# Four attention blocks on one core: q and k in fp32 over 128 channels, heads in four row groups, maxima by a matmul of their own

## The reference

```python
h = group_norm(x, 32 groups) * gn_w + gn_b        # eps 1e-5; 1e-6 in the last block
q, k, v = wq h + bq, wk h + bk, wv h + bv         # per token, 128 -> 128
p = softmax(q^T k / sqrt(d))                      # blocks 0-2: 8 heads, d = 16; block 3: 1 head, d = 128
x = wp (p v) + bp + x
```

## Time and profile before

| | |
|---|---|
| runs | 115.41, 115.49, 114.85 us |
| profiled execution, first to last instruction (span) | 112.7 us; its own run time is not listed beside it |
| instructions | 2178 |
| PE matmuls, weight loads | 99.7 us (88%), 80.1 us (71%), 774 each |
| DVE, ACT, POOL busy | 77.9 us (69%), 78.4 us (70%), 7.9 us (7%) |
| mean granted TensorE clock | 0.997 |
| moved by DMA | 2.12 MB, 16 engines' mean share above a half only in two of the first three of 40 slices |

### The profile page before, as it was taken

One profiled execution on the slowest core, in us unless ns is written; L12 is line 12 of the kernel. 1 busy time (PEld: TensorE's weight loads), 2 busy tenths in 40 slices (PEclk: granted clock), 3 DMA queues, 4 the chain that ended last, 5 costly groups with the idle time before them and its releaser, 6 DMA issues.

```text
span 112.7 us, 2178 instructions
## 1 busy us (share of the span) xinstructions
PE 99.7 (88%) x774; PEld 80.1 (71%) x774; DVE 77.9 (69%) x192; ACT 78.4 (70%) x168; POOL 7.9 (7%) x17
## 2 busy tenths in 40 slices
PE   6999689979969998599999899979998898789891
PEld 6998468756955967378877678768977565579770
DVE  5467789273992879826699357997869516786862
ACT  4387569998677937989828996377999995024520
POOL 8421000000001000010000100010000000102000
PEclk9999999999999999999999999999999999999998
DMA  2950000000000000000000000000000000000011
GB/s 65 333 214 0 0 0 6 0 0 0 3 9 0 0 0 0 0 0 6 0 0 0 0 6 0 0 0 0 6 0 0 0 0 9 0 3 0 0 47 47
DMA packets 1882, 2.12 MB, mean 19 GB/s; under 512 B 336, under 2 KB 1232, under 8 KB 1872
## 3 DMA queue, kind: packets, MB, share of 16 engines
q1 hardware_dynamic: 1584, 1.84, 4.8%
q10 hardware_dynamic: 288, 0.15, 0.6%
HBM read 1.73 MB, written 0.26 MB: 18 GB/s over the span
## 4 chain that ended last, share of the span: by engine, by line
PE 58%; ACT 20%; DVE 14%; issue 4%; DVEq 0%; ACTq 0%
ACT probs L668 9%; PE ps_o L563 9%; PE ps_t L550 9%; ACT q_heads L658 8%; PE ps_w L492 7%; PE ps_o L469 6%; DVE neg_max L761 6%; PE ps_w L520 4%; PE ps_w L510 4%; PE ps_w L511 3%; PE ps_m L498 2%; DVE q_heads L755 2%; PE ps_m L537 2%; PE ps_m L477 2%; PE ps_m L609 2%
## 5 line engine op out<-in xcount | busy, mean ns | idle before, releaser
L761 DVE TENSOR_REDUCE neg_max<-ps_w 128x2 f32<-128x512 f32 x48 | 31.0, 685 | 6.8 <-PE ps_w L520 6.7
L668 ACT ACTIVATE probs<-ps_t 128x512 f32<-128x512 f32 x48 | 27.5, 597 | 4.1 <-PE ps_t L550 3.3
L550 PE MATMUL ps_t<-q_heads,k_pairs 128*128 128x256 f32 x96 | 20.8, 313 | 3.1 <-ACT probs L668 1.6
L520 PE MATMUL ps_w<-k_pairs,q_heads 128*128 128x256 f32 x96 | 20.4, 314 | 1.8 <-DVE neg_max L761 0.8
L658 ACT ACTIVATE q_heads<-ps_m 1x256 fp32r<-1x256 f32 x48 | 17.9, 373 | 5.0 <-PE ps_m L537 4.1
L550 PEld LDWEIGHTS ps_t<-q_heads,k_pairs 128*128 128x128 f32 x96 | 14.1, 189 | 7.0 <-ACT q_heads L658 4.3
L520 PEld LDWEIGHTS ps_w<-k_pairs,q_heads 128*128 128x128 f32 x96 | 13.9, 189 | 5.5 <-issue 2.4
L510 PE MATMUL ps_w<-qk_high,select 128*128 128x256 f32 x48 | 12.9, 300 | 0.9 <-DVE qk_low L726 0.5
L563 PE MATMUL ps_o<-probs,v_heads 128*32 128x256 f32 x192 | 12.8, 385 | 0.9 <-ACT probs L668 0.9
L511 PE MATMUL ps_w<-qk_low,select 128*128 128x256 f32 x48 | 11.8, 279 | 0.0
L423 POOL TENSOR_TENSOR grp<-grp,const 128x1 f32<-128x1 f32 x8 | 4.5, 558 | 93.8 <-DVE grp L715 93.8
(11 more groups left out here) (62 smaller groups left out, 130.2 us busy)
## 6 DMA issues: line engine op xcount, KB each, us to landing
w<-in_w SPq DMA_DIRECT2D x4, 256.0 KB, 4.9
xs<-in_x SPq DMA_DIRECT2D x2, 128.0 KB, 3.1
selections<-in_selections SPq DMA_DIRECT2D x1, 256.0 KB, 4.0
out<-xs SPq DMA_DIRECT2D x4, 64.0 KB, 1.6
const<-in_constants ACTq DMA_DIRECT2D x1, 137.0 KB, 3.1
vec<-in_vectors ACTq DMA_DIRECT2D x1, 12.0 KB, 3.5
```

The costliest lines, as they stand in the source:

```text
L520: last = mm(ps_w[w_slot[step]][:, qc * T:(qc + 1) * T], q_heads[b][:, i, qc * CHUNK:(qc + 1) * CHUNK], k_pairs[b][:, i // 2, :], start=Tru ...
L550: last = mm(dst, k_pairs[b][:, pair, keys], q_heads[b][:, i, :], start=True, stop=True)
L668: nc.scalar.activation(probs[:, i, :, :].rearrange("p c t -> p (c t)"), src, ACT.Exp, scale=SCALE).then_inc(exps_done, 1)
L761: nc.vector.tensor_reduce(neg_max[b][:, i // 2, :, QUAD * (i % 2)], ps_w[w_slot["scores", l, b, i]][:, :].rearrange("p (c t) -> p c t", c= ...
```

## The change

The planner goes; the file holds a fixed list (`PLAN`) of the same form of steps in one order, and each step that fills PSUM names its banks out of eight that all kinds share. Before a PE step fills a bank it waits for the step that emptied it (`bank_free`). The steps change as follows.

- Statistics: `sum_x` on DVE at the start only (later the residual accumulates the sum as it writes x), `negate_sum` on DVE, `sum_squares` on ACT (Square with accumulation, over x and two padding columns that carry eps), one fp32 `group_means` matmul. variance, power on POOL and normalise as before.
- q and k stay fp32 in 128 channels, with no high and low parts and no placing. k is stored twice: `store_k_even` (ACT) with the channels of odd heads zeroed, `store_k_odd` (DVE) with those of even heads zeroed. A group of 32 rows holds an even and an odd head, so a matmul over 32 rows gives one head's scores. `scores` and `scores_t` work on four heads at once, in four row groups and four PSUM banks, each 8 fp32 matmuls (K = 32).
- Maxima: four heads' maxima are laid in columns 0, 32, 64, 96 of `neg_max`, one `turn_max` transposes them for four heads (two transposes), `store_max` (ACT) copies 128x256 to `max_rows` (fp32r), and `add_max` adds them into the four banks of scores_t by four fp32r matmuls (K = 32, 512 columns) with a matrix whose first row of each group is ones.
- `attend` as before, but `probs` is one tile per image. Its result is transposed in 32x32 blocks by DVE (`turn_out`), divided, transposed back by DVE (`turn_back`), without ACT and PE. v's bias is folded into the output's bias (`fold_out`, `add_out`), so `store_attended` goes.
- `store_v` is on ACT. In the last layer wp wv is multiplied once (`fold_wv`, `store_wv`), so the layer has no `project_out`.
- Start: x of image 1 is issued by ACT between constants (67 KB in place of 137 KB) and vectors; SP issues x of image 0, w0, an identity of 64 KB, w1 to w3 and wv of the last layer. The selections (256 KB) and their four ACT steps go. POOL's memsets are ten. Filler matmuls are 9, none after the start.

Cut to its core:

```diff
-mm(dst, select[:, pair, 2 * k, :], qk_high[b][:, k, :], start=True, stop=False)
-last = mm(dst, select[:, pair, 2 * k + 1, :], qk_low[b][:, k, :], start=False, stop=True)
...
+elif kind == "scores":
+    bank_free(step)
+    pe.wait_ge(q_stored, nth("store_q", l, b))
...
+    keys = k_odd[b] if i else k_even[b]
+    for qc in range(NCH):
+        for g in range(PER):
+            of = slice(ROWS * g, ROWS * (g + 1))
+            last = mm(ps(*step, g)[:, qc * T:(qc + 1) * T], q[b][of, qc * CHUNK:(qc + 1) * CHUNK],
+                      keys[of, :], start=True, stop=True)
+    last.then_inc(scores_done, 1)
+elif kind == "scores_t":
...
+    for kc in range(NCH):
+        for g in range(PER):
+            of = slice(ROWS * g, ROWS * (g + 1))
+            mm(ps(*step, g)[:, kc * T:(kc + 1) * T], keys[of, kc * CHUNK:(kc + 1) * CHUNK], q[b][of, :],
+               start=kc == 0, stop=False, skip_group_check=True)
+elif kind == "add_max":
...
+    pe.wait_ge(max_stored, nth("store_max", l, b, i))
+    for g in range(PER):
+        of = slice(ROWS * g, ROWS * (g + 1))
+        dst = ps("scores_t", l, b, i, g)[:, :].rearrange("p (c t) -> p c t", c=NCH)
+        row = max_rows[b][of, i:i + 1, :].to_broadcast([ROWS, NCH, T])
+        last = mm(dst, first_rows[of, :], row, start=False, stop=True, skip_group_check=True)
+    last.then_inc(max_added, 1)
...
+elif kind == "sum_squares":
+    nc.scalar.activation(squares[b][:, 0:cols], xs[b][:, 0:cols], ACT.Square,
+                         accum_out=mom[b][:, 2:3]).then_inc(x_squared, 1)
+elif kind == "store_k_even":
+        last = nc.scalar.activation(k_even[b][:, :], src, ACT.Identity,
+                                    bias=bias[:, l, FK_EVEN:FK_EVEN + 1], scale=even)
+elif kind == "store_max":
+    nc.scalar.activation(max_rows[b][:, i, :], ps("turn_max", l, b, i)[:, 0:T],
+                         ACT.Copy).then_inc(max_stored, 1)
...
+elif kind == "store_k_odd":
+    ts(k_odd[b][:, :], ps("project_k", l, b)[:, 0:T], bias[:, l, FK:FK + 1], odd,
+       ALU.add, ALU.mult).then_inc(k_odd_stored, 1)
+elif kind == "turn_out":
+    dve.wait_ge(attended, nth("attend", l, b, i))
+    nc.vector.transpose(turned[b][:, i, :, :].rearrange("p n d -> p (n d)"),
+                        ps("attend", l, b, i)[:, 0:T]).then_inc(out_turned, 1)
```

More of the change, by code:

```diff
@@ L60 @@
 NCH = T // CHUNK
+NB = T // ROWS
 GROUP = 4
-EPS = [1e-5, 1e-5, 1e-5, 1e-6]
+BANKS = 8
+EPS = 1e-5
+EPS_LAST = 1e-6
 SCALE = DH ** -0.5
 SCALE_ONE = C ** -0.5
-WORK, SLOTS = 3, 2
 GN_W, GN_B, BQ, BK, BV, BP = range(6)
 NVEC = 6
[L71 to L119, removed]
@@ L123 @@
[L123 to L140, removed]
@@ new lines @@
+store_max 0 1 1; divide 0 0 0; store_max 0 1 0; add_max 0 1 1; turn_back 0 0 0; fold_out 0 0 0 1; exps 0 1 5
+project_out 0 0 0 6; add_out 0 0 0; exps 0 1 7; scores_t 0 1 0 0 3 1 2; residual 0 0 0; exps 0 1 6
+negate_sum 1 0 0; sum_squares 1 0 0; exps 0 1 4; add_max 0 1 0; group_means 1 0 0 7; exps 0 1 3
+fold_bias 1 0 0 6; variance 1 0 0; exps 0 1 0; rsqrt 1 0 0; attend 0 1 1 2; scale_w 1 0 0; normalise 1 0 0
+exps 0 1 1; add_bias 1 0 0; project_q 1 0 0 7; exps 0 1 2; turn_out 0 1 1; project_k 1 0 0 3; store_q 1 0 0
@@ new lines @@
+divide 1 1 1; project_k 2 0 0 1; store_q 2 0 0; attend 1 1 0 5; store_k_even 2 0 0; store_k_odd 2 0 0
+scores 2 0 0 2 0 7 6; turn_out 1 1 0; divide 1 1 0; scores 2 0 1 3 4 1 5; row_max 2 0 0; turn_back 1 1 0
+row_max 2 0 2; project_out 1 1 0 2; row_max 2 0 1; project_v 2 0 0 7; residual 1 1 0; row_max 2 0 3
+sum_squares 2 1 0; store_v 2 0 0; negate_sum 2 1 0; row_max 2 0 5; turn_max 2 0 0 6; group_means 2 1 0 2
+store_max 2 0 0; row_max 2 0 6; scores_t 2 0 0 0 7 4 6; variance 2 1 0; row_max 2 0 7; rsqrt 2 1 0
@@ new lines @@
+row_max 2 0 4; add_max 2 0 0; normalise 2 1 0; exps 2 0 2; turn_max 2 0 1 3; project_k 2 1 0 2; exps 2 0 0
+project_q 2 1 0 4; store_max 2 0 1; store_k_even 2 1 0; project_v 2 1 0 0; store_q 2 1 0; store_k_odd 2 1 0
+store_v 2 1 0; scores 2 1 0 1 5 3 4; exps 2 0 3; exps 2 0 1; row_max 2 1 0; scores_t 2 0 1 2 0 6 7
+row_max 2 1 3; row_max 2 1 2; add_max 2 0 1; attend 2 0 0 4; exps 2 0 7; row_max 2 1 1; exps 2 0 5
+turn_max 2 1 0 5; turn_out 2 0 0; exps 2 0 6; scores 2 1 1 1 3 7 0; store_max 2 1 0; exps 2 0 4; row_max 2 1 7
@@ new lines @@
+scores_t 2 1 0 4 6 5 2; row_max 2 1 6; row_max 2 1 4; add_max 2 1 0; attend 2 0 1 7; exps 2 1 0; row_max 2 1 5
+exps 2 1 3; turn_max 2 1 1 3; turn_out 2 0 1; exps 2 1 1; scores_t 2 1 1 0 1 4 2; divide 2 0 1; store_max 2 1 1
+exps 2 1 2; divide 2 0 0; add_max 2 1 1; turn_back 2 0 0; attend 2 1 0 5; exps 2 1 5; exps 2 1 6
+fold_out 2 0 0 1; turn_out 2 1 0; exps 2 1 4; project_out 2 0 0 3; add_out 2 0 0; exps 2 1 7; residual 2 0 0
+divide 2 1 0; attend 2 1 1 2; sum_squares 3 0 0; negate_sum 3 0 0; group_means 3 0 0 3; turn_out 2 1 1
```

844 lines of the change are left out of this document (351 added, 493 removed).

## The result

The changed kernel takes 98.56 us (median of 4 runs, 96.88 to 99.58) against 115.13 us for the kernel before (113.99 to 115.49, the new run among them). The forecast was 97.0 us. The profiled execution took 96.88 us with a span of 95.1 us; the walk had given 95.0. It was the fastest of the four and the only one with a mean granted clock of 1.000; the others took 97.83, 99.30 and 99.58 us with 0.964, 0.982 and 0.965.

What follows compares the result with a forecast made beforehand. Two images of dependent steps sharing three engines, none full, were taken as the bound; 81.4 us to the last layer's projection plus 13.6 made a 95.0 us span, 97.7 with 2.7 added, said as 97.0 for overlaps; range 87 to 109.

Steps and rivals of the forecast that it cites:

- the walk: New plan's layer 1 order followed step by step with row durations; with start and end, a span of 95.0 us.
- What bounds the kernel before: No engine full; work removed from one engine alone only moves waits, from the chain or all three shortens the period.
- The row-group step: scores and scores_t on PE: sixteen fp32 rows, four at once, 0.94 us plus ways in and out and loads, 1.2 us.
- rival C: Row groups run one after another on PE, a step 3.8 + 0.2 us: 143 us (115 to 150), chance 0.07.
- Rival B: Weight loads of the row groups don't overlap, a step 1.8 us: 108 us (102 to 111), chance 0.15.
- The new prices: New ACT, DVE and PE rows: transposes 0.45, max store 0.38, k_even 0.55, squares 0.47 + 0.19, k_odd 0.48, add_max 0.4 us.
- rival D: Square isn't in Exp's table set, so each sum_squares brings two loads of 1.28 us: 109 us, chance 0.04.
- The period: Layer 1 of both images, from scores(1,0,0) to the next layer's scores: 25.9 us, against 30.5 and 31.4 before.
- The start: Up to the first row_max, predicted at 10.45 us instead of 13.48, 3 us earlier.
- The end: From the last layer's projection to the end: 13.6 us, 1.7 off the last layer's 15.3.
- The 2.7 us around the span: Median of the kernel before, 115.41 us, less its profiled span of 112.7; taken to stay and added to 95.0.
- Rival A: Banks and queues give no waits beyond PE's 21 us a period and 1.5: 87 us (85 to 92), chance 0.13.

Runs made afterwards that it cites:

- b1: The kernel before with the 48 placing matmuls of the low parts left out (TensorE work only): 113.86 us, ratio 0.985 to the kernel before.
- b2: The kernel before with only one of the two one-row stores of each store_max on ScalarE, exponent scaled by 0.1: 110.98 us, ratio 0.966.
- e7: The changed kernel with each scores and scores_t matmul over all 128 rows, so none share the array, exponent scaled by 0.1: median 153.5 us.
- e1: The changed kernel with the two loops of scores and scores_t swapped, so neighbouring matmuls share a row group: 95.82 and 97.52 us.
- e3: The changed kernel with three more filler matmuls at the start: three runs at 95.14 to 95.45 us, three at 98.67 to 99.63, ratio 0.821 by the first three.
- e2: The changed kernel with q and both copies of k stored in fp32r, low bits left out: median 96.94 us (94.63 to 104.09).
- e10: The changed kernel with store_k_odd moved from VectorE to ScalarE: median 97.49 us, ratio 0.847 to the kernel before.
- e4: The changed kernel without turn_max, store_max and add_max, exponent scaled by 0.1: median 98.15 us (96.27 to 98.41).
- e8: The changed kernel with q and k in fp32r and two filler matmuls ahead of each scores and scores_t: median 93.49 us, ratio 0.803.

## Why the prediction was right, and where its terms were off

- **What bounds the kernel before.** Right in the main. b1 and b2 returned 0.3 and 0.4 of the work taken from one engine, so such work doesn't only move waits; the change took from all three at once and returned 17.6 us of span. How these divide between the placing, the stores of the maxima, the turns and the statistics, no run separates. (In that working the turns that leave PE, 24 and 36 rows at 0.12, are 7.2 us, not 6.6; nothing rests on it.)
- **The row-group step.** Right in kind, a little high: 1.03 us without a change of mode behind it and 1.08 with one, against 1.2. It is 0.94 of matmuls and 0.1 of everything else; the change of mode is 0.05 of it, where the ways in and out had been counted at 0.08 and 0.06 from attend. e7 shows that rival C's price (a step of 3.46 us, 3.8 forecast; 153.5 us, 143 forecast) was real and its condition false. Rival B fell with the step: sixteen weight loads of 128 columns take 0.74 us together, where B had them one after another, 1.6.
- **The new prices.** DVE transposes 0.44 (0.45), max store 0.387 (0.38), k_even 0.573 (0.55), squares 0.417 and a read of 0.186 (0.66 together), k_odd 0.544 (0.48), add_max 0.43 (0.4). One table load: rival D fell.
- **The period.** 24.5 us against 25.9. The walk's landmarks came earlier by a growing amount: the second scores_t at 41.85 - 32.90 = 8.95 (9.15), image 1's second scores at 47.71 - 32.90 = 14.8 (15.3), the last add_max at 53.62 - 32.90 = 20.7 (21.7 to begin with, 22.1 done). Two terms were too high. One is the step, by 0.12 to 0.17 us each time. The other is the exps, walked at 0.60 from start to start where four of them come 0.49 apart: 0.3 us less for each group of four. The first group shows it: walked from 7.3 to 9.7, it ran from 7.18 to 9.24 (40.08 and 42.14 less 32.90). ACT's sum shows it as well, 13.4 us against 15.9, of which 16 x 0.11 = 1.8. The prediction had named such overlaps and taken 0.7 us off for them in the whole kernel. How the 1.4 us divide between the two was not separated. Layer 2, which was walked only by analogy, was 24.8 us to the last projection instead of 23.5, and gave most of it back; why is open.
- **The start.** The mis-sized term of the other sign: first row_max at 12.21 instead of 10.45, because the six projection rows took 2.91 us at half pace. The text had this as +2 in the walk's own range. In e1 and e3 it came at 10.51, the forecast.
- **The end.** 12.9 us against 13.6.
- **Sum.** Span 95.1 against 95.0 is luck in its closeness, by five errors that cancel: +1.8 at the start, about -0.8 from the first row_max to scores(1,0,0) (20.7 us against 21.5) and -1.4 in layer 1, +1.3 in layer 2, -0.7 at the end. The 2.7 us around the span was 1.8 in the profiled execution, and is 1.8 in the kernel before too where one execution has both (114.46 us with a span of 112.7, beside e7): the prediction had set the median against a span that there goes with 114.46. The median of 98.56 lies above 96.88 since the other three executions, all with a lower granted clock, took 1.0 to 2.7 us more; that the clock is the cause is not shown, as the one at 0.982 was slower than the one at 0.964.
- **Rival A** (a period of PE's 21 us and 1.5) would have been too low for this kernel. e2's period at full clock, 22.5 us, reached that length only with most of the scores' work gone, so PE's sum alone isn't the period.

## What to carry to other kernels

Walk the new order step by step with durations from rows of the old trace, and use the nearest relative for a mode that the trace doesn't show: column groups told here what row groups would do. Price a step's removal by what the queue does next: of work taken from one engine of a balanced kernel a third came back in time (b1), of work that stood between two waits nearly half (b2), and of VectorE's k_odd nothing (e10). When PE gets less work, look at the granted clock before judging the edit, and compare stretches that ran at the same clock: e4 as a whole seemed to gain nothing, and in its stretch at full clock it gained 1.6 us.

## What the hardware showed beside that

- Row groups overlap even when neighbouring matmuls are of the same group: sixteen rows in 1.04 us grouped (e1) against 1.03 us in turn, 1.10 against 1.08 with attend behind them.
- With less TensorE work the granted clock was lower: mean 0.964 to 1.000 in the four executions of the changed kernel, 0.80 to 0.891 in e2, where short scores lay between idle stretches, 0.979 to 0.981 in e8 with fillers. Two attends took 3.64 us at 1.2 GHz.
- At the start the same six projection rows took 2.91 or 1.53 us from run to run while the granted clock in the profile read 1.00 in both (changed kernel, e1); the distances of starts tell the pace there, the clock column doesn't.
